# Routing stage of a transformer kernel: three buffers for rows and places, two small steps on VectorE

## What is computed

```python
x = x + _L1_attn_ref(_layernorm(x), ...)        # linear attention
...
xt = x.reshape(-1, d)                            # of _layernorm(x)
probs = jax.nn.softmax((xt @ Wr + br) / TEMP, axis=-1)
w, idx = jax.lax.top_k(probs, 2)                 # two experts for a token, with weights
w = w / jnp.clip(jnp.sum(w, axis=-1, keepdims=True), 1e-09)
...
h = gelu(einsum('td,edh->teh', xt, W1) + b1); o = einsum('teh,eho->teo', h, W2) + b2
y = xt + sum over experts of w * o
```

## Time and profile before

| | before |
|---|---|
| median of 3 runs, us | 624.8 |
| profiled execution, us | 624.82 |
| its span, us | 621.9 |
| busy: PE / DVE / ACT / POOL | 80% / 66% / 56% / 59% |
| mean granted clock of TensorE | 0.91 |
| second stage | about 314 to 478 us |

### The profile page before, as it was taken

The page is one execution under the profiler, slowest core; times in us unless marked ns, Lnnn a source line. Parts: engine busy times, 40 slices in busy tenths (PEclk is TensorE's granted clock), DMA queues, the critical chain, the costliest instruction groups (busy, mean ns, idle before and its releaser), DMA issues.

```text
span 621.9 us, 14283 instructions
## 1 busy us (share of the span) xinstructions
PE 500.3 (80%) x4164; PEld 336.5 (54%) x4164; DVE 408.5 (66%) x1038; ACT 345.3 (56%) x733; POOL 369.7 (59%) x637
## 2 busy tenths in 40 slices
PE   4767899999999999988868887787644899889900
PEld 4523455555555555444645565555433799888800
DVE  6767868788788888852347988887746255444206
ACT  2026757777777777667236676665521366555500
POOL 3545767777777777332331577776674177777750
PEclk8769989999999999999899989996855999999955
DMA  3767532433443343200071001110113333333229
GB/s 101 169 164 192 123 102 88 117 95 95 104 104 104 104 98 99 73 4 3 2 227 50 19 32 36 34 33 31 36 35 99 79 84 96 95 93 95 71 70 342
DMA packets 66459, 55.95 MB, mean 90 GB/s; under 512 B 8523, under 2 KB 59872, under 8 KB 66400
## 3 DMA queue, kind: packets, MB, share of 16 engines
q1 hardware_dynamic: 58584, 45.13, 27.4%
q0 software_dynamic: 4608, 8.47, 4.0%
q10 hardware_dynamic: 3208, 1.65, 1.1%
HBM read 30.54 MB, written 25.71 MB: 90 GB/s over the span
## 4 chain that ended last, share of the span: by engine, by line
PE 12%; issue 12%; POOL 9%; DMA 6%; DVE 6%; ACT 3%; SPq 1%; POOLq 1%; DVEq 0%; ACTq 0%
POOL disp L1114 4%; POOL back L1628 3%; PE p_qkv L1758 2%; DMA disp<-pay,pos 2%; DMA back<-XN2T,rows 2%; PE p_tb L1737 2%; DMA own<-back 1%; ACT rl L1406 1%; DMA rows<-disp 1%; PE p_tb L1444 1%; POOL root L1132 1%; DVE mv L1346 1%; PE p_u L1773 1%; PE p_h L1773 1%; PE p_u L1467 1%
## 5 line engine op out<-in xcount | busy, mean ns | idle before, releaser
L456 DVE TENSOR_REDUCE negmax<-p_dve 128x4 f32<-128x1024 f32 x128 | 156.2, 1223 | 47.5 <-PE p_dve L682 46.1
L574 ACT ACTIVATE probs<-p_exp 128x1024 f32<-128x1024 f32 x128 | 130.7, 1021 | 29.9 <-PE p_exp L656 29.4
L1628 POOL DMA_INDIRECT back<-XN2T,rows x80 | 82.4, 1029 | 41.7 <-issue 22.9
L1114 POOL DMA_INDIRECT disp<-pay,pos x64 | 68.8, 1074 | 37.0 <-DVE pos L1321 22.8
L673 PE MATMUL p_out<-probs,V 128*32 128x256 f32 x1024 | 75.6, 390 | 0.0
L656 PE MATMUL p_exp<-QS,KS 64*128 64x256 bf16 x512 | 50.8, 277 | 10.9 <-ACT probs L574 5.8
L682 PE MATMUL p_dve<-KS,QS 61*128 61x256 bf16 x512 | 51.5, 281 | 9.8 <-DVE negmax L456 9.7
L1718 ACT ACTIVATE hid<-p_qkv,own 128x128 f32<-128x128 f32 x160 | 45.7, 368 | 22.5 <-PE p_qkv L1758 21.9
L1758 PE MATMUL p_qkv<-XN2T,own 128*128 128x128 f32 x320 | 43.0, 277 | 2.5 <-ACT XN2T L1708 2.5
L1682 DVE COPY own<-expert 128x578 f32 x80 | 34.9, 478 | 11.7 <-issue 11.5
L1758 PEld LDWEIGHTS p_qkv<-XN2T,own 128*128 128x128 f32 x320 | 38.8, 191 | 3.7 <-ACT XN2T L1708 3.4
(11 more groups left out here) (267 smaller groups left out, 1205.6 us busy)
## 6 DMA issues: line engine op xcount, KB each, us to landing
scratch<-part SPq DMA_DIRECT2D x32, 192.0 KB, 2.1
KS<-scratch SPq DMA_DIRECT2D x32, 192.0 KB, 3.2
QS<-scratch SPq DMA_DIRECT2D x32, 192.0 KB, 4.4
rows<-disp SPq DMA_DIRECT2D x80, 65.0 KB, 1.9
scratch<-part SPq DMA_DIRECT2D x32, 128.0 KB, 1.9
own<-back SPq DMA_DIRECT2D x8, 512.0 KB, 6.7
expert<-in_W_dram SPq DMA_DIRECT2D x1, 2064.0 KB, 8.9
scratch<-part SPq DMA_DIRECT2D x32, 64.0 KB, 1.8
```

The source lines that it names most:

```text
L456: dve.tensor_reduce(negmax[q][:, i, :, 2 * hp:2 * hp + 2], p_dve[buf][:, :].rearrange("p (v w k) -> p v w k", v=HALF, k=S), AX.X, ALU.max, ...
L574: act.activation(probs[s % 4][:, :, :, :].rearrange("p v w q -> p (v w q)"), p_exp[:, :], ACT.Exp)\
L1114: pool.indirect_dma_start(out=disp, out_offset=bass.IndirectOffsetOnAxis(ap=pos[q][:, i, k:k + 1], axis=0), in_=pay[q][:, k, i, :], in_off ...
L1628: pool.indirect_dma_start(out=back, out_offset=bass.IndirectOffsetOnAxis(ap=rows[r][:, h, D + 1:ROW].bitcast(U32), axis=0), in_=y[r][:, h, :],
```

## The change

`pay`, `pos` and the `sent` signals get three buffers (STORED = 3), picked by the block modulo 3. All waits for an earlier use of them reach back three blocks in place of two. The step that advances the row numbers is no longer on POOL ahead of a block's last scatter, but on DVE in iteration b + 5 behind `sel`, for the block itself and from block 3 on, in steps of three blocks. The step that adds epsilon goes from POOL, where it came right before the power, to the end of DVE's iteration behind the second `bn_stats`, with the waits that it had; POOL waits for its signal `var_s` and then takes the power. The expert stage waits for three `sent` signals. The core of the diff:

```diff
+STORED = 3
...
-        pay = [tmp(f"pay_{r}", [P, TOP, TT, ROW]) for r in range(PAIR)]
+        pay = [tmp(f"pay_{r}", [P, TOP, TT, ROW]) for r in range(STORED)]
...
-        pos = [tmp(f"pos_{r}", [P, TT, TOP], U32) for r in range(PAIR)]
+        pos = [tmp(f"pos_{r}", [P, TT, TOP], U32) for r in range(STORED)]
...
-        st3, power_s, nw, nm3 = sig("st3"), sig("power_s", 2), sig("nw", 4), sig("nm3", 2)
+        st3, power_s, nw, nm3 = sig("st3"), sig("power_s"), sig("nw", 4), sig("nm3", 2)
+        var_s = sig("var_s")
...
-        sent = [sig(f"sent{q}", 16 * TT * TOP) for q in range(PAIR)]
+        sent = [sig(f"sent{q}", 16 * TT * TOP) for q in range(STORED)]
...
             def root_power(m, q):
 
                 if not (active(m, 0) or active(m, 3)):
                     return
-                if active(m, 0):
-                    pool.wait_ge(st3.sem, st3.at(m))
-                if active(m, 3):
-                    pool.wait_ge(st4.sem, st4.at(m - 3))
-                if active(m, PAIR):
-                    pool.wait_ge(nm3.sem, nm3.at(m - PAIR))
-                if active(m, 3 + PAIR):
-                    pool.wait_ge(nm4.sem, nm4.at(m - 3 - PAIR))
+                pool.wait_ge(var_s.sem, var_s.at(m))
                 steady(pool, t)
-                pool.tensor_scalar(root[q][:, 3, :], mv[q][:, :, 2], 1.0 / D, EPS, ALU.mult, ALU.add).then_inc(power_s.sem, 1)
-                pool.wait_ge(power_s.sem, power_s.at(m, 1))
                 pool.tensor_tensor(root[q][:, 0, :], root[q][:, 3, :], t["power"][:, :], ALU.pow).then_inc(power_s.sem, 1)
...
-                    scatter(o, 0, 0)
+                    scatter(n - 5, 0, 0)
                 root_power(n, r)
...
-                if active(n, 4 + PAIR) and active(n, 4):
-                    b = n - 4
-                    pool.wait_ge(sent[b % PAIR].sem, sent[b % PAIR].at(b // PAIR - 1))
-                    steady(pool, t)
-                    pool.tensor_scalar(pay[r][:, :, :, D + 1].bitcast(I32), pay[r][:, :, :, D + 1].bitcast(I32), float(PAIR * TOP * TT), None, ALU.add)\
-                        .then_inc(ids_up.sem, 1)
...
+                    if b >= STORED:
+                        q = b % STORED
+                        dve.wait_ge(sent[q].sem, sent[q].at(b // STORED - 1))
+                        ids = pay[q][:, :, :, D + 1].bitcast(I32)
+                        dve.tensor_scalar(ids, ids, float(STORED * TOP * TT), None, ALU.add).then_inc(ids_up.sem, 1)
...
+                if active(n, 0) or active(n, 3):
+                    if active(n, 0):
+                        dve.wait_ge(st3.sem, st3.at(n))
+                    if active(n, 3):
+                        dve.wait_ge(st4.sem, st4.at(n - 3))
+                    if active(n, PAIR):
+                        dve.wait_ge(nm3.sem, nm3.at(n - PAIR))
+                    if active(n, 3 + PAIR):
+                        dve.wait_ge(nm4.sem, nm4.at(n - 3 - PAIR))
+                    dve.tensor_scalar(root[r][:, 3, :], mv[r][:, :, 2], 1.0 / D, EPS, ALU.mult, ALU.add).then_inc(var_s.sem, 1)
...
-                    if b >= PAIR:
-                        act.wait_ge(sent[b % PAIR].sem, sent[b % PAIR].at(b // PAIR - 1))
-                    if res.due(b - PAIR):
-                        act.wait_ge(res.sem, res.at(b - PAIR))
+                    if b >= STORED:
+                        act.wait_ge(sent[b % STORED].sem, sent[b % STORED].at(b // STORED - 1))
+                    if res.due(b - STORED):
+                        act.wait_ge(res.sem, res.at(b - STORED))
```

More of the change, by code:

```diff
@@ L1092, in _ @@
                 pool.memset(KVones[r][:, :, D:D + H], 1.0).then_inc(s2.sem, 1)
-            for r in range(PAIR):
+            for r in range(STORED):
                 pool.iota(pay[r][:, :, :, D + 1].bitcast(I32), pattern=[[1, TOP], [TOP, TT]], base=r * TOP * TT, channel_multiplier=TOP * TT * B,
@@ L1111, in _, with scatter @@
             pool.tensor_copy(bparts[:, 2, :], brest[:, :]).then_inc(bsplit.sem, 1)
-            def scatter(q, i, k):
+            def scatter(b, i, k):
+                q = b % STORED
                 pool.indirect_dma_start(out=disp, out_offset=bass.IndirectOffsetOnAxis(ap=pos[q][:, i, k:k + 1], axis=0),
@@ L1138, in iteration @@
                     pool.wait_ge(pos_s.sem, pos_s.at(b))
[L1139 to L1140 removed]
+                    if ids_up.due(b - STORED, 1):
+                        pool.wait_ge(ids_up.sem, ids_up.at(b - STORED))
                     steady(pool, t)
[L1142 removed]
+                    scatter(n - 5, 0, 0)
                 root_power(n, r)
                 if active(n, 5):
[L1145 removed]
+                    scatter(n - 5, 0, 1)
                 if active(n, 5):
[L1147 to L1153 removed]
+                    scatter(n - 5, 1, 0)
                 if active(n, 5):
[L1155 removed]
+                    scatter(n - 5, 1, 1)
             pipeline(pool, iteration, 5)
@@ L1312, in iteration @@
                     dve.wait_ge(nm4.sem, nm4.at(b))
-                    if b >= PAIR:
-                        dve.wait_ge(sent[b % PAIR].sem, sent[b % PAIR].at(b // PAIR - 1))
-                    dve.tensor_tensor(pay[o][:, :, :, D], odds[:, :, :],
+                    if b >= STORED:
+                        dve.wait_ge(sent[b % STORED].sem, sent[b % STORED].at(b // STORED - 1))
+                    dve.tensor_tensor(pay[b % STORED][:, :, :, D], odds[:, :, :],
                                       wide(z[:, :].rearrange("p (o i) -> p o i", o=1), [P, TOP, TT]), ALU.mult).then_inc(pos_s.sem, 1)
@@ L1320, in iteration @@
                     with nc.allow_low_precision(reason="one term of each sum is not zero, and it is a whole number"):
-                        dve.tensor_reduce(pos[o][:, :, :], mine[:, :, :, :], AX.X, ALU.add).then_inc(pos_s.sem, 1)
+                        dve.tensor_reduce(pos[b % STORED][:, :, :], mine[:, :, :, :], AX.X, ALU.add).then_inc(pos_s.sem, 1)
                 if active(n, 5):
                     b = n - 5
-                    dve.tensor_tensor(X[:, bass.ds(2 * b, 2), :], X[:, bass.ds(2 * b, 2), :], pay[o][:, 0, :, 0:D], ALU.add).then_inc(res.sem, 1)
+                    dve.tensor_tensor(X[:, bass.ds(2 * b, 2), :], X[:, bass.ds(2 * b, 2), :], pay[b % STORED][:, 0, :, 0:D], ALU.add).then_inc(res.sem, 1)
                 if active(n, 3):
@@ L1362, in iteration @@
                     if at(b, 0):
-                        act.wait_ge(s2.sem, 4)
+                        act.wait_ge(s2.sem, PAIR + STORED)
                     act.activation(KVones[o][:, :, 0:D], p_qkv[:, :].rearrange("p (i c) -> p i c", i=TT)[:, :, 2 * D:3 * D], ACT.Copy)\
@@ L1492, in iteration @@
                         pe.wait_ge(x4T_s.sem, x4T_s.at(b - 1))
-                    turn(p_tb, pay[r][:, 0, :, :]).then_inc(x4T_p.sem, 1)
+                    turn(p_tb, pay[b % STORED][:, 0, :, :]).then_inc(x4T_p.sem, 1)
                 if active(n, 4):
@@ L1633, in expert_sp @@
     def expert_sp(sp):
-        for q in range(PAIR):
-            sp.wait_ge(t["sent"][q].sem, t["sent"][q].at(B // PAIR - 1))
+        for q in range(STORED):
+            sp.wait_ge(t["sent"][q].sem, t["sent"][q].at((B - 1 - q) // STORED))
         sp.wait_ge(w["loaded3"].sem, w["loaded3"].at(0))
```

7 lines of the change are left out of this document (5 added, 2 removed).

## The result

The changed kernel took 607.39 us (median of 4 runs, 605.99 to 609.49), the kernel before 624.5 beside it (620.85 to 625.89). The ratio is 0.9738, 95% interval 0.9685 to 0.979. The forecast of 611.2 is 3.8 us above this median and 1.7 us above the profiled execution's 609.49.

What follows compares the result with a forecast made beforehand. It took a two-block loop of packing, places, scatters and landing as the bound, VectorE next. From 624.8 us, -6.95 - 2.55 - 4.65 + 0.6 = -13.55 gave 611.2 us, range 606.5 to 618.

Steps and rivals of the forecast that it cites:

- A, a middle iteration: Routing stage: 7.00 us of VectorE work plus epsilon gives 7.50 for blocks 1 and 2, 7.60 from block 3.
- Epsilon was taken at 0.50: Epsilon on VectorE behind the second bn_stats: bounds 0.15 and 0.50 us, taken as held to the scatter's end, 0.50.
- the 0.45 of idle: VectorE's wait for the power before the root's first step in a short 7.45 us iteration; claimed to go.
- The row numbers at 0.1: Row-number step on VectorE behind sel, from block 3: bounds 0.1 and 0.6 us, taken at 0.1.
- The first rival: Both moved steps blocked to the scatter's end: row numbers cost 0.6, not 0.1, 13 times; 617.7 us; chance 0.15.
- The rival that epsilon isn't held: Epsilon costs 0.15 on VectorE, power still waited for: iterations of 7.25, total 607.0 us; chance 0.18.
- B, blocks 0 to 10: Routing blocks 0 to 10: 82.75 us before, 75.8 after, a gain of 6.95.
- C, blocks 10 to 12: Routing blocks 10 to 12: 17.15 us before, 14.6 after, a gain of 2.55.
- the allowance of 0.4 for the clock: Blocks 10 to 12: 0.4 us added to each block's 6.9 of VectorE work, as TensorE may be partly slow.
- the clock falls all the same: TensorE's clock still falls: gain of blocks 10 to 12 lost and as much again, 614.7 us; chance 0.13.
- D, blocks 12 to 15: Routing blocks 12 to 15: 23.50 us before, gain 4.65, mostly 3.96 from block 15's packing starting at once.
- E, the start: Iterations 0 to 4, no scatter beside epsilon: 0.15 to 0.2 each, a loss of 0.6 us.

Runs made afterwards that it cites:

- e1: Changed kernel with both moved steps back on GpSimd, three buffers kept: 609.27 us, ratio 0.9816 to the kernel before.
- e2: Changed kernel with two buffers in place of three, both steps still moved to VectorE: 617.69 us, ratio 0.9936 to the kernel before.
- e7: Changed kernel plus idle TensorE turns behind the last new block, five more at the queries' place from iteration 19: 646.41 us, ratio 0.9941 to the kernel before.
- e11: Changed kernel plus idle TensorE turns where the recurrence's last products stood, none at the queries' place: 605.20 us, ratio 0.9736 to the kernel before.
- e12: e11's kernel with epsilon in two-operand form behind the next iteration's sum of X, root steps one place later: 609.76 us, ratio 0.9794 to the kernel before.
- e5: Changed kernel with four buffers in place of three: 641.94 us, ratio 0.9899 to the kernel before on that chip.
- e4: Changed kernel with only the row-number step back on GpSimd: 609.76 us, ratio 0.9816 to the kernel before.
- e8: Changed kernel with nothing altered, run again on a second chip: 610.32 us, ratio 0.983 to the kernel before.
- e10: Changed kernel with epsilon in two-operand form on VectorE and the row numbers back on GpSimd: 607.05 us, ratio 0.9781 to the kernel before.
- e3: Changed kernel with only the epsilon step back on GpSimd: 610.71 us, ratio 0.9824 to the kernel before.
- e6: Changed kernel with epsilon reading from a tile (two tensor operands), on the 649.5 us chip: 642.73 us, ratio 0.9898 to the kernel before.
- e9: Changed kernel with epsilon reading from a tile (two tensor operands), on the second chip: 609.62 us, ratio 0.9791 to the kernel before.

## Why the prediction was right

*The bound.* The loop of packing, places, scatters and landing was what made the long iterations, and the third buffer removed it: e1 alone has them gone, e2 alone keeps them. VectorE took over, as forecast.

*A, a middle iteration.* Forecast 7.50 and 7.60, measured 7.23 to 7.36. Two of its terms were mis-sized. Epsilon was taken at 0.50, from a scatter's end; its price is 0.26. The step that should have given the size was read by its recorded duration, and neither the hold (0.2 in the middle blocks, recorded) nor the duration alone (0.15) is what a full queue pays: the start of the next step behind it is. And the 0.45 of idle in the earlier trace rows was worth a little more: from `KVm` to the root's first step it was 0.75 before and 0.25 after, so 0.50. The row numbers at 0.1 were right (0.05 to 0.1). By these 7.45 - 0.50 + 0.26 + 0.05 to 0.1 is 7.26 to 7.31.

The first rival, both steps blocked to the scatter's end, falls: the row numbers took 0.16 in blocks 3 to 11 and 0.29 at most. The rival that epsilon isn't held gave 7.25 and 607.0, and its number is the nearest to both the spacing and the median, though its mechanism is not the one seen: the step is held, and it doesn't matter. The page of the Trainium skill "SBUF — State Buffer", section "Who interferes with whom", would have the second engine fully blocked. The epsilon step's record bears a hold out in part, 0.37 for 0.17, but it ends with or before the scatter, and the next VectorE step starts 0.07 behind its start.

*B, blocks 0 to 10.* Forecast 75.8, measured 73.25: ten times some 0.25, which A explains.

*C, blocks 10 to 12.* Forecast 14.6, measured 17.63 in the profiled execution and 15.40 in the second. The step that failed is the allowance of 0.4 for the clock. It was sized for a fall that follows a late packing; without any late packing the clock still fell, behind a window in which TensorE was busy for 2.42 of 4 us. Idle turns in that place prevent the fall (e7, e11, e12), but e5 kept 1.00 at the same busy time without them, so what brings the clock down there stays open in part. The rival "the clock falls all the same" named this, with C's gain lost and as much again. C's gain is lost in one execution, two thirds of it kept in the other. With the clock at 1.00, e11 gives 14.18 and e5 14.35, so VectorE's 6.9 per block plus little was a sound count.

*D, blocks 12 to 15.* Forecast 18.85, measured 19.12 and 18.61. Block 15's packing follows its last factor at once, as the prediction's list asked.

*E, the start.* Forecast +0.6; the five iterations ahead take 26.61 to 26.62 for 26.02, in e4, e8 and e10 alike, and 26.02 to 26.03 in e1 and e3, which have epsilon on GpSimd. In the profiled execution of the changed kernel they took 3.6 us more, with a low clock beside it, and the first stage, which no line of the diff touches, ended 3.4 us earlier. The two cancel.

So B came out 2.5 us shorter than forecast and C 3.0 longer, the two met in the sum, and most of the agreement of the profiled execution is owed to that: it is luck. The 1.7 us that are left are mostly two parts that the prediction took as fixed: 0.9 behind block 15's places, and 1.1 outside the span, 1.8 for 2.9. The median of 607.39 lies 3.8 below the forecast, within its range.

## What to carry to other kernels

When a buffer's reuse makes every second iteration long, count the loop from the last reader's landing back to the first writer, and look at what the next engine's queue holds without its waits: that is the new spacing, and one more buffer reaches it. Price a small step by the distance between its neighbours' starts, not by its recorded duration, and ask whether it reads what the step right before it writes. Once two engines are full within a tenth or two of a microsecond, as VectorE and GpSimd in e10, moving a step between them gave next to nothing; look then for a stretch where TensorE has less work and its clock falls.

## What the runs showed of the hardware

- A VectorE step of four columns recorded with 0.37 beside a scatter and one with 0.16 cost its queue the same: the next step starts 0.07 to 0.08 behind either. Reading a result written by the step right before cost 0.18 on top (0.52 from start to start, for 0.34).
- Beside a scatter, a `tensor_scalar` of four columns was recorded longer only where it started 0.23 to 0.44 us before the scatter's end, and it ended 0.02 to 0.04 before that end. This holds in every trace here: epsilon 0.36 to 0.42 (0.37 in the rows above, 1.02 us into a scatter of 1.42), the row numbers (int32) 0.29 in the change's block 15 and 0.37 to 0.40 in three blocks of e6. Where they started 0.45 or more before the end, as the row numbers mostly did, they took 0.15 to 0.17. Epsilon in the form with two tensors, at the same place beside the scatter in e9, took 0.16.
- Five or six idle turns of TensorE in an iteration, put behind the last new block, kept the granted clock at 1.00 until 448 us, where it had fallen at 421. Four runs with them took 604.7 to 606.3 us, four without 607.7 to 612.9.
- The same kernel before took 621.6, 621.8 and 622.3 us on three chips and 649.5 on a fourth. e5's trace on that fourth has waits of up to 3.6 us without a releaser; kernels with three or four buffers gained only 0.6 to 1.0% there.
